# A four-layer transformer kernel: order of the work around one expert layer and one bias table

## The reference

```
L1_ffn:  logits = x @ router_w.T ; top 2 of 8 experts ; probs = softmax(top 2)
         h = gelu(x @ w1[e].T + b1[e]) ; y = h @ w2[e].T + b2[e]        # F = 512
         out = sum over the 2 chosen experts of probs * y
L2_cond: attention with 16 heads of 64, q and k normalised, and
         pos  = -1023 .. 1023
         t    = silu(ln(pos @ w0 + b0, g0)) ; t = silu(ln(t @ w1 + b1, g1)) ; t = t @ w2 + b2
         bias[head, i, j] = t[i - j + 1023, head]
L0_cond: attention with a given bias; both attentions begin with q, k, v = ln(x) @ W
L2_ffn:  q = x @ Wq ; scores against 64 keys per half ; top 8 of the products of both halves
```

## Time and profile before

| | us |
|---|---|
| median of 3 runs | 3097.19 (3096.54 to 3098.55) |
| the profiled run's own time | 3096.48 |
| its span in the trace | 3094.8 |
| qkv_phase of layer 0 | from 18 to about 140 |
| route_phase of L1_ffn | 1099 to 1214.5 |
| kept_experts_phase of L1_ffn | 1214.5 to 1423 |
| qkv_phase of layer 2 | 1433 to 1590 |
| core_phase of layer 2 | 1591 to 2110 |
| product_key_phase | 2199 to 2616 |

### The profile page before, as it was taken

One profiled execution on the slowest core, in us unless ns is written; L12 is line 12 of the kernel. 1 busy time (PEld: TensorE's weight loads), 2 busy tenths in 40 slices (PEclk: granted clock), 3 DMA queues, 4 the chain that ended last, 5 costly groups with the idle time before them and its releaser, 6 DMA issues. The chain is left out here.

```text
span 3094.8 us, 56173 instructions
## 1 busy us (share of the span) xinstructions
PE 2512.4 (81%) x16472; PEld 2048.1 (66%) x16472; DVE 1589.5 (51%) x4387; ACT 1318.4 (43%) x3132; POOL 940.5 (30%) x1173
## 2 busy tenths in 40 slices
PE   4799999988786944774779999998599998883795
PEld 2477777767686843673447777776577776772685
DVE  3366666644115353113866666654488886535111
ACT  2365666753221421222445666674344442152221
POOL 0132333311105445342433333331233431445002
PEclk9999999998897966998989999999899999895898
DMA  7022222202565364211111222320200001145585
GB/s 264 31 63 84 69 82 71 81 26 109 187 227 133 103 220 148 83 53 54 32 61 66 70 84 62 92 62 15 78 1 1 0 0 46 60 133 191 209 304 177
DMA packets 150617, 296.57 MB, mean 96 GB/s; under 512 B 24918, under 2 KB 110167, under 8 KB 144321
## 3 DMA queue, kind: packets, MB, share of 16 engines
q1 hardware_dynamic: 136112, 254.53, 24.2%
q0 software_dynamic: 14352, 40.22, 4.2%
HBM read 240.25 MB, written 64.56 MB: 98 GB/s over the span
## 5 line engine op out<-in xcount | busy, mean ns | idle before, releaser
L787 DVE CUSTOM_DVE_ANT_0 prob_l<-ps_l,bias_l,nsn 128x1024 f32<-128x1024 f32 (+3 forms) x256 | 276.7, 1081 | 113.1 <-DVEq L786 65.3
L787 DVE CUSTOM_DVE_ANT_0 cur_sb<-ps_h,bias_s,nsn 128x128 f32<-128x128 f32 (+3 forms) x256 | 139.6, 545 | 241.5 <-DVEq L786 241.0
L862 ACT ACTIVATE prob_l<-prob_l,nmax 128x1024 f32<-128x1024 f32 (+3 forms) x256 | 252.0, 985 | 2.0 <-DVE nmax L787 1.5
L718 PE MATMUL ps_l<-khi,stage 128*128 128x512 f32 (+3 forms) x512 | 240.9, 471 | 0.0
L682 POOL COPY nsn<-nsn 128x4 f32 (+1 forms) x128 | 24.1, 188 | 713.2 <-DVE diff L804 570.9
L724 PE MATMUL ps_pt<-ident_sb,prob_l 128*128 128x128 f32 x1664 | 231.7, 276 | 5.3 <-ACT cur_sb L846 2.2
L846 ACT ACTIVATE cur_sb<-ps_pt 128x128 f32<-128x128 f32 (+3 forms) x256 | 111.1, 434 | 267.9 <-PE ps_pt L724 267.8
L691 POOL TENSOR_TENSOR stage<-qo,stage 64x256 fp32r<-64x256 f32 x256 | 201.3, 786 | 46.4 <-POOLq L690 46.4
L724 PEld LDWEIGHTS ps_pt<-ident_sb,prob_l 128*128 128x128 f32 x1664 | 186.6, 141 | 29.5 <-ACT cur_sb L846 13.8
L287 PE MATMUL ps_q<-wf,xnT 128*128 128x512 f32 (+1 forms) x384 | 146.6, 535 | 52.7 <-ACT xnT L323 52.7
L2248 POOL TENSOR_TENSOR ss<-simx,sim 128x4096 f32<-128x4096 f32 x16 | 113.4, 7085 | 238.2 <-DVE simx L2396 238.2
(11 more groups left out here) (342 smaller groups left out, 6263.4 us busy)
## 6 DMA issues: line engine op xcount, KB each, us to landing
mlp_ws<-in_L_ffn_experts_dram SPq DMA_DIRECT2D x39, 2052.0 KB, 7.4
xs<-slot_rows SPq DMA_DIRECT2D x156, 128.0 KB, 2.1
slot_outputs<-ys SPq DMA_DIRECT2D x156, 128.0 KB, 1.9
slot_rows<-zero_sb SPq DMA_DIRECT2D x1, 16384.0 KB, 51.4
bias_l<-in_fside_16xSxS_dram SPq DMA_DIRECT2D x16, 512.0 KB, 3.4
mlp_w<-in_L_ffn_experts_dram SPq DMA_DIRECT2D x8, 1024.0 KB, 18.8
bias_by_partition<-bias_table POOLq DMA_DIRECT2D x1, 8192.0 KB, 36.6
bias_l<-bias_by_partition SPq DMA_DIRECT2D x16, 512.0 KB, 3.3
```

The lines of the kernel that those rows point to most:

```text
L718: ins = pe.matmul(out, stage[:, b, s, x.h % 2, x.h // 2, :], att[part][:, b * S + lo:b * S + hi], start=False, stop=part == "klo", skip_gr ...
L787: dve.tensor_tensor_reduce(out=spans(x, prob), in0=scored(x), in1=spans(x, bias), scale=-1.0, scalar=nsn[:, b, s, h:h + 1], op0=ALU.add, o ...
L862: act.activation(prob[x.s][:, x.h, 0:x.W], prob[x.s][:, x.h, 0:x.W], ACT.Exp, bias=nmax[:, x.b, x.s, x.h:x.h + 1], scale=-1.0, accum_out=r ...
```

## The change

There are five edits.

A. qkv_phase: PE waits for `folded` in `products` of tile 0 and not at its start. ACT's two foldings stand behind the root of tile 1, and DVE's behind `normalised` of tile 0, at step 1.

B. kept_experts_phase: PE's stages are `(0, transposes), (1, hidden), (2, outputs)`. The one copy on POOL's queue is eight copies of two heads each on SP's queue; each stands behind the load of an even tile from 4 to 18. SP's pipeline is unrolled. core_phase waits for all eight.

C. route_phase with a table: the eight expert loads and the rows' load on SP each wait for `logits` of a tile (0 to 8); the table's store stands behind them as before.

D. The same phase: the second half of the table (from `second_layer` on DVE, from the second root on ACT, from the second `turn` on PE) is called after each engine's pipeline.

E. product_key_phase: SP loads `wq` ahead of its wait for the memset. PE waits for the keys in `queries` of tile 0.

```diff
@@ qkv_phase
-            pe.wait_ge(folded, 2 * KD)
             def products(t, u):
+                if isinstance(t, int) and t == 0:
+                    pe.wait_ge(folded, 2 * KD)
...
-            stages = [(0, combine), (0, moments), (1, normalised)]
+            stages = [(0, combine), (0, moments), (1, normalised), (0, folded_weights)]
@@ core_phase
-                sp.wait_ge(bias_made, 16)
+                sp.wait_ge(bias_made, 16 * (H // 2))
@@ route_phase
+            if experts is not None and table:
+                for e, (dst, src_) in enumerate(experts.loads):
+                    sp.wait_ge(dve_l.sem, dve_l.after("logits", min(e, NT - 1)))
+                    sp.dma_start(dst, src_).then_inc(experts.sem, 16)
+                experts.load_columns(sp)
...
-                if t == 6:
-                    table.second_layer(dve)
-                if t == 7:
-                    table.normalise(dve, 2)
-                if t == 9:
-                    table.turned_half(dve, 2)
...
+            if table:
+                table.second_layer(dve)
+                table.normalise(dve, 2)
+                table.turned_half(dve, 2)
@@ kept_experts_phase
+            def spread(h):
+
+                sp.dma_start(spread_dram[h:h + 2], bass.AP(table_dram.tensor, table_dram.offset + h * (S + P) + P - 1,
+                                                           [[S + P, 2], [-1, P], [1, S]])).then_inc(spread_done, 16)
+
+            def load_and_spread(t, u):
+                load(t, u)
+                if t % 2 == 0 and t >= 4 and t < 4 + H:
+                    spread(t - 4)
...
-            pipeline(sp, n_tiles, 4, (0, load), (4, store))
+            unrolled(sp, n_tiles, 4, (0, load_and_spread), (4, store))
...
-            gp.dma_start(spread_dram, bass.AP(table_dram.tensor, table_dram.offset + P - 1,
-                                              [[S + P, H], [-1, P], [1, S]])).then_inc(spread_done, 16)
...
-            pipeline(pe, n_tiles, 4, (0, transposes), (2, outputs), (1, hidden))
+            pipeline(pe, n_tiles, 4, (0, transposes), (1, hidden), (2, outputs))
@@ product_key_phase
-            sp.wait_ge(zeroed, 1)
-            for dst, src in first:
+            for i, (dst, src) in enumerate(first):
+                if i == 1:
+                    sp.wait_ge(zeroed, 1)
                 sp.dma_start(dst, src).then_inc(keys_in, 16)
...
-            pe.wait_ge(keys_in, 16 * len(first))
             def queries(t, u):
+                if isinstance(t, int) and t == 0:
+                    pe.wait_ge(keys_in, 16 * len(first))
```

More of the change, by code:

```diff
@@ L309, in _ @@
                 s.open(act)
-            act.wait_ge(weights, 16 * len(loads))
-            for k in range(KD):
-                act.activation(wf[:, k, 0:NULL], w[:, k, :], ACT.Copy, scale=gcol[:, k:k + 1]).then_inc(folded, 1)
             def root(t, u):
@@ L318, in root @@
                 act.activation(sd[:, u, :], mv[:, u, 1:2], ACT.Sqrt, bias=c["eps"][:, 0:1]).then_inc(act_0.sem, 1)
+                if isinstance(t, int) and t == 1:
+                    act.wait_ge(weights, 16 * len(loads))
+                    for k in range(KD):
+                        act.activation(wf[:, k, 0:NULL], w[:, k, :], ACT.Copy, scale=gcol[:, k:k + 1]).then_inc(folded, 1)
             def transposed_x(t, u):
@@ L1314, in _ @@
                 act.activation(z[:, 1, :], z[:, 1, :], ACT.Exp).then_inc(exped, 1)
+            if table:
+                table.root(act, 2)
+                table.silu(act, 2)
+                table.turned_first(act, 2)
+                table.last_bias(act)
         @block.vector
```

64 lines of the change are left out of this document (30 added, 34 removed).

## The result

The changed kernel takes 3140.43 us (median of 4 runs, 3138.49 to 3141.25) and the kernel before 3097.87 (4 runs, 3096.54 to 3102.07). The ratio is 1.0134, with a 95% interval of 1.0117 to 1.0152: slower by 1.3%. The forecast was 3147, slower. The profiled run's span is 3139.6 us against 3094.8.

The account below looks back on a forecast made before the run. PE work in fixed order, with one wait per tile for hT, bound the expert loop, the largest touched phase. 3096.48 + 60.3 - 5.0 - 3.8 - 1.5 = 3146.5, median 0.7 above: 3147 us; range 3040 to 3170.

Parts of the forecast that it names:

- The likeliest case: Expert loop of layer 1: each two-head piece moves on two engines, 20.2 us, and delays tile loads; +60.3 us; chance 0.70.
- Rival (a): Expert loop: pieces go over all sixteen engines, so PE's new order wins its whole gain; 3045 us median; chance 0.19.
- Two of the signs: Expert loop, profile after: xs loads landing over 15 us; PE waiting for xs some 20 us every second tile.
- The term of the loop: Expert loop of layer 1: two-engine pieces delay tile loads, PE's new order gains only in the last 20 tiles; +60.3 us.
- The period behind the pieces: Expert loop, after the eighth piece: 3.97 us a tile without the hT wait, 21 steps, 83.4 us.
- a clock that starts low: Expert loop, after the last piece: PE's granted clock starts low, adding some 3 us.
- Part 1: Expert loop: PE's hidden ahead of outputs removes the wait for hT; worth 41.4 us if nothing else stops it.
- Part 3: Layer 1 routing: table's second half behind the routing, expert loads held back; next phase starts 5.0 us sooner.
- The loads' gate: Layer 1 routing: expert loads held behind the logits stop crowding the first gathers; 3.9 us sooner for second_layer.
- Part 4: qkv phases: folding behind the first moments starts products sooner; -2.9 us in layer 0, -0.9 in layer 2, -3.8 in all.
- the products then run PE-bound: qkv phases: PE bounds the products, so an earlier start is an earlier end; -3.8 us rests on it.
- Part 5: Product-key phase: only queries(0) waits for keys, and wq no longer for POOL's memset; -1.5 us.

Follow-up runs that it names:

- The first experiment: The changed kernel with each 1 MB piece taking 16 heads by 16 partitions, not 2 by 128; 3028.10 us, ratio to the kernel before 0.9765.

## Why the prediction was right, and where its steps were off

**The likeliest case came true by its own mechanism.** A piece moved as if on two engines, at the rate of a lone engine (158 ns a row), and in its queue's order. The piece period was 21.25 against 21.6. The first experiment, with nothing but the pattern changed, and the one with four heads show the outermost count as the cause; the one on POOL's queue speaks for the queue's order as what stops the loads, by three loads that landed ahead of the piece beside them. Rival (a) had the right sign for a pattern of sixteen and was 13 to 17 us off: 3028 to 3032, where 3045 was given, as the loop gained 54.5 and not 41.4. What the prediction left out is that SP itself would stand, 15 us and more behind most pieces. Two of the signs that it gave for being right were off: PE waited 12.3 us at most and not some 20 (a period of 21.6 less the work of two tiles leaves 14), and the loads landed in 12.6 in the median and not over 15. The counts 2, 4 and 16, with 21.25, 11.3 and at most 5.8 us a piece, agree with the rule that was cited from the Trainium skill ("DMA: Bandwidth & Descriptors", section "Why a DMA increments its semaphore by 16 and not by 1"), which the trace of before could not try. The three loads that landed ahead of a piece in another queue (5.9 to 7.0 us) agree with what its section "Queues, rings and completion order" says, that a DMA engine takes turns between the queues that have work for it.

**The term of the loop was 7.3 us too large.** Two sizes were off. The period behind the pieces was 3.73, not 3.97: 21 x 0.24 = 5.0. I had taken the wait of 1.03 from the period of 5.0 and did not see that starts around a wait are late too; the runs show 1.27 a tile. And transposes(19) came 175.9 after the phase's start (1383.55 - 1207.61) where 177.7 were forecast: 1.8. That leaves 0.5. The 3 us that had been added for a clock that starts low were about right: the step from the transposes at 1383.55 to the next ones took 6.50 us and not 3.73, so 2.8 more, at a granted clock of 0.50 in its first 4 us.

**Part 1, the order: the mechanism right, the number by luck.** 41.4 was forecast and the order alone gave 41.6, but as a sum of two errors: the gain was larger (1.41 a period in the mean, 1.14 forecast), and the stop at the crowded load (9.50, and 2.39 before) had been left out.

**Part 3: the sum right, its parts not.** -4.7 against -5.0, and the start of second_layer 18.6 earlier against 18.7. The loads' gate gave 0.1 to 2.5 of it, not 3.9, and the second half 15.0 to 17.4, not 14.8; so the nearness of the sum is in part luck. The gathers' landing did fall with gated loads, to 3.6 in the median of the changed kernel's first nine (7.3 in the earlier trace rows), but not for the ones that count: combine(0) waits for the second gather, which landed 6.4 us after its issue where it had taken 7.6. It was the later ones that came down, to 2.8 for the sixth.

**Part 4: right in layer 0 (-2.5 against -2.9); in layer 2 right at the start and drowned at the end.** The step that failed is "the products then run PE-bound", at a length that was taken as fixed: DVE has more work there than PE, PE stands for it, and the length moved by 4 us with the granted clock, which was put at nothing. Within each of the two lengths the edit is worth its 1 us. In the one profile of the changed kernel, a long one, it read +2.1.

**Part 5: the step from start to end failed.** queries(0) came 1.36 us sooner, and none of it reached the end, which came 1.0 later after the memset. The cause stays open.

The account in spans: 50.0 forecast, less 7.3 in the loop, plus 0.3 in the routing, 0.4 and 3.0 in the two qkv phases and 3.3 in the product-key phase, less 4.9 in phases that the change does not touch: 44.8, the difference of the two spans. The medians differ by 42.6. So the total, 3140 against 3147, is nearer than its parts: 7.0 too much hope in the small phases stands against 7.3 too much cost in the loop, and the 4.9 are chance.

## What to carry to other kernels

Before a copy is cut in pieces, look at the outermost count of each piece's pattern: keep it at sixteen, as here, and cut along an inner count. A slow transfer in a queue stops every small one behind it, and then the engine that issues, so what the piece costs is what stands behind it. An edit that lets the first instruction of a phase start sooner may be worth nothing at its end: see first which engine paces the phase, and how far its length moves by itself.

## What the runs showed of the hardware that was not expected

An issuing engine can stand on a DMA: stores behind two-headed pieces took 15.06 to 17.20 us to issue on SP, where they took 0.34 behind the last of them, and the eighth 1 MB piece on POOL's queue came 30.6 us after the seventh. The 8 MB copy on sixteen engines was issued in 1.10 us. That a queue's room had ended would explain both, and no run here shows it.

The same two-headed pieces ran one at a time in SP's queue (DMA share 0.21, 21.25 us each) and side by side in POOL's (0.94 of sixteen engines, seven pieces in some 40 us).

A matmul stream that is never broken runs faster than its broken parts suggest: 3.73 us a tile, where the period less the visible wait gave 3.97.
